# A graph-attention layer on one Trainium2 core: x loaded before the edge lists, edge keys by broadcast transfers instead of matmuls, and the scores of a head pair in one run of six banks

## The chip, the cores and the metric

The kernel runs on one core of one Trainium2 chip. The metric is device time in microseconds of the slowest core (here the only one); lower is better. A core has TensorE (PE, matmuls), VectorE (DVE), ScalarE (ACT), GpSimd (POOL), SyncE (SP, which here only issues transfers), and 16 transfer engines. Each engine works through its own instructions in order; they meet at semaphores.

## What is computed

A pre-normalised graph attention layer on 384 nodes with 1024 features and 16 heads of 64, all in float32:

```python
h = jnp.maximum(_layernorm(x, axis=-1), 0.0)
q = h @ wq.T + bq;  k = h @ wk.T + bk;  v = h @ wv.T + bv
q2 = (q @ wiq.T + biq).reshape(N, H, D).transpose(1, 0, 2)   # k2, v2 alike
mask = jnp.full((N, N), -jnp.inf)
mask = mask.at[src, dst].set(softplus(edge_type_weights)[edge_type - 1])   # 6528 edges, last one wins
# the diagonal is set to softplus(weights)[3] where no edge has set it
scores = jnp.einsum('hnd,hmd->hnm', q2, k2) * scale + mask[None]
attn = softmax(scores)
out = einsum('hnm,hmd->hnd', attn, v2).transpose(1, 0, 2).reshape(N, 1024)
return x + out @ wo.T + bo
```

## The kernel before

**Number format.** Every large product is made of three fp32r matmuls, high by high, low by high and high by low (`products`, L752 to L760). So each operand is split: ACT copies it to a rounded high part, and DVE or POOL subtracts that from the exact value for the low part. The weights come as 56 slabs of 128 x 1024 float32 (512 KB each) through three raw buffers; SP loads slab s when the low part of slab s - 3 is made (`wait_lo`, L232), ACT splits off the high part (L390), and the low part is made by DVE (L627, slabs 1 up to 37) or POOL (L325, L335: slab 0 in two halves, and from slab 38 on).

**The start.** SP issues the edge rows, the edge columns, then x (tile 0 of 128 nodes in halves, tiles 1 and 2 whole), slabs 0 and 1, the fill of two tables of cells in HBM, slab 2 and so on (L259 to L270). POOL makes constants. DVE turns the edge lists to numbers and computes a key per edge, src * 384 + dst (L514 to L524), then the statistics of x (L591 to L597); POOL takes the power for 1/std (L318), DVE makes the shift (L535), and ACT applies Relu(scale * x + shift) (L417); the last half tile is done by DVE (L605, L609). PE runs 13 warming matmuls (L819), turns h around in 24 transposes (L829), three to a feature block k, and multiplies block k - 2 in between; ACT and DVE split each transposed block (L421, L640) in three PSUM banks used in turn. Between the low parts 3 and 4 DVE makes the values of the edges (`edge_values`, L565 to L583).

**Edges.** When several edges hit the same cell, the last must win. For each of 51 tiles of 128 edges, PE brings the 128 keys as a row to all partitions by one matmul against a selecting column (`keys`, L762, four tiles to a unit and a bank), and DVE compares it with the keys as a column and counts later equal ones (L547). Edges with a later equal one are sent to a dump cell (L556, L559). POOL then scatters the values, one transfer of 128 per tile, in two chains on two tables (L346, L352); each chain's scatters wait for one another. Finally both tables are read back (L362) and DVE joins them to the mask (`build_mask`, L629).

**The projections.** Step s of the main loop deals with slab s + 3 and the output tile of slab s, on ACT (L428 to L450) and on DVE (L647 to L667): DVE takes the comparison of edge unit s + 1, the low part of slab s + 3, then the low part of tile s (L615). PE works through v (tiles 0 to 7), then v2 (8 slabs), q, k (16 tiles), then q2 and k2 by pairs of heads. PE may begin tile t only when DVE's low part of tile t - 2 is done (L787), since two banks take turns.

**The pairs.** For each pair j of heads, PE computes scores in three chunks n of 128 query nodes, both heads side by side (L873, 64 rows of the array each), into four banks used in turn (`score_bank`, L155). Around them it places matmuls of the next q2 and k2 tiles (`filler`), transposes of the previous pair's probabilities (L885, into banks 5 to 7), and their products with v2 (L900, L901), which need the transposed block's high part from ACT (L468) and low part from DVE (L692). The order on PE is: chunks 0 and 1, filler, transposes of head h, filler, values of h, chunk 2, transposes of h + 1, filler, values of h + 1 (L951 to L968). On DVE: the maxima of chunks 0 and 1 (`max_part`, L678, one per head and chunk), the sum for the last head of the pair before (`head_part`, L701), reciprocals (L688), the three pt_lo, and later the two maxima of chunk 2. On ACT: exponentials of chunk 0 (L461), the copy of the finished pair (L454, which waits for that sum), exponentials of chunk 1, three pt_hi, and later those of chunk 2. The output projection is drawn into the last pairs.

Of the kernel before, what the change touches and what calls it, by code (L numbers as in the profile page):

```python
# [12 lines left out]
F32 = mybir.dt.float32  # L13
# [7 lines left out]
P = 128  # L21
N = 384
# [30 lines left out]
WARM = 13  # L53
# [16 lines left out]
def gat_kernel(nc, slabs, x, edge_cols, edge_rows, edge_weights, biases, bo, out):  # L70
    with ExitStack() as ctx:
# [32 lines left out]
        rows_i = sb("rows_i", [P, P], I32)  # L104
        rows = sb("rows", [P, P], F16)
# [13 lines left out]
        select = sb("select", [P, ET], F16)  # L119
# [25 lines left out]

        def cell_rows(c):
# [4 lines left out]
        key_bank = bank[0:2]  # L151
        h_bank = [bank[5], bank[4], bank[7]]
        tile_bank = bank[3:5]
        v2_bank = [bank[5:8], bank[0:3]]
        score_bank = [bank[0], bank[1], bank[7], bank[2]]  # L155
        pt_bank = bank[5:8]
# [10 lines left out]
        edges_in, small_in, y_in = sem("edges_in"), sem("small_in"), sem("y_in")  # L167
        x_half_in = sem("x_half_in")
        x_in = [sem(f"x_in{t}") for t in range(NT)]
        slab_in = [sem(f"slab_in{r}") for r in range(RAW)]  # L170
        const_step, iota_ok, select_ok, above_ok = sem("const_step"), sem("iota_ok"), sem("select_ok"), sem("above_ok")
        dump_ok, ident_ok, fill_ok = sem("dump_ok"), sem("ident_ok"), sem("fill_ok")
        edge_step, rows_ok, keys_done, later_ok, value_ok = (
            sem("edge_step"), sem("rows_ok"), sem("keys_done"), sem("later_ok"), sem("value_ok"))
# [19 lines left out]
        y_ok, out_done, out_ok, stored = sem("y_ok"), sem("out_done"), sem("out_ok"), sem("stored")  # L194

# [28 lines left out]
        def lo_by_vector(s):  # L224

            return 1 <= s < LO_ALL
# [31 lines left out]
        def _(sp_eng):  # L258
            sp_eng.dma_start(rows_i[:], edge_rows).then_inc(edges_in, 16)  # L259
            sp_eng.dma_start(cols_i[:], edge_cols).then_inc(edges_in, 16)  # L260

            sp_eng.dma_start(x_sb[:, 0, 0:HALF], x[0:P, 0:HALF]).then_inc(x_half_in, 16)
            sp_eng.dma_start(x_sb[:, 0, HALF:F], x[0:P, HALF:F]).then_inc(x_in[0], 16)
            for t in range(1, NT):
                sp_eng.dma_start(x_sb[:, t, :], x[t * P:(t + 1) * P, :]).then_inc(x_in[t], 16)
            for s in range(SLABS):
                if s >= RAW:

                    wait_lo(sp_eng, s - RAW)
                sp_eng.dma_start(raw[:, s % RAW, :], slabs[s]).then_inc(slab_in[s % RAW], 16)  # L270
                if s == 1:
                    for c in range(2):
                        sp_eng.wait_ge(fill_ok, c + 1)
                        sp_eng.dma_start(cell_rows(c), prob[:, c]).then_inc(filled, 16)
                if s == Q0 + 2:

                    sp_eng.wait_ge(h_turned, KT)
                    for t in range(NT):
                        sp_eng.dma_start(y[:, t, :], x[t * P:(t + 1) * P, :]).then_inc(y_in, 16)
# [7 lines left out]
        def _(pool):  # L287
# [3 lines left out]
            nc.gpsimd.memset(select[:], 0.0).then_inc(const_step, 1)  # L291
# [8 lines left out]
            pool.wait_ge(const_step, 4)  # L300

            nc.gpsimd.affine_select(out=select[:], in_=select[:], compare_op=ALU.not_equal, fill=float(N),
                                    base=0, pattern=[[-1, ET]], channel_multiplier=1).then_inc(const_step, 1)
            pool.wait_ge(const_step, 5)
            nc.gpsimd.affine_select(out=select[:], in_=select[:], compare_op=ALU.not_equal, fill=1.0,
                                    base=-DST_ROW, pattern=[[-1, ET]], channel_multiplier=1).then_inc(select_ok, 1)
# [13 lines left out]

            def split_lo(s):
# [10 lines left out]
            for b in range(2):  # L332
                half = slice(b * HALF, (b + 1) * HALF)
                pool.wait_ge((half_hi, slab_hi)[b], 1)
                nc.gpsimd.tensor_tensor(w_lo[:, 0, half], raw[:, 0, half], w_hi[:, 0, half].bitcast(F32),  # L335
                                        ALU.subtract).then_inc((half_lo, slab_lo)[b], 1)
# [18 lines left out]

            done = 0
# [28 lines left out]
        def _(act):  # L385
# [18 lines left out]
            act.dma_start(ew[:], edge_weights.rearrange("(a n) -> a n", a=1).to_broadcast([P, 4])).then_inc(small_in, 16)  # L404
            act.dma_start(bias[:], biases).then_inc(small_in, 16)
            act.wait_ge(sp_in, 1)
            nc.scalar.activation(sp[:, 2, :], sp[:, 1, :], ACT.Exp).then_inc(sp_exp, 1)
            act.wait_ge(sp_exp, 1)
            nc.scalar.activation(sp[:, 3, :], sp[:, 2, :], ACT.Ln, bias=1.0).then_inc(sp_ln, 1)

# [16 lines left out]
            act.wait_ge(small_in, 32)  # L427
            for s in range(QK0 + TILES_AHEAD):  # L428
                split_hi(s + AHEAD)
                if s < VV0:  # L430
                    tile_hi_part(s)
# [33 lines left out]
            def pt_hi_part(h, m):  # L465

                act.wait_ge(pt_done, h * NT + m + 1)
                nc.scalar.activation(pt_hi[:, m, :], pt_bank[m][:, 0:N], ACT.Copy).then_inc(pt_hi_ok, 1)  # L468
# [42 lines left out]
        def _(dve):  # L511

            dve.wait_ge(edges_in, 32)
# [502 lines left out]
```

## Time and profile before

| | |
|---|---|
| median of 3 runs | 312.71 us (312.55 to 312.86) |
| the profiled execution | 312.73 us |
| its span, first to last instruction | 311.2 us |
| busy: PE / DVE / ACT / POOL | 297.2 / 182.2 / 154.6 / 148.0 us |
| share of the chain that ended last: PE / DVE / ACT / DMA | 88 / 5 / 3 / 2% |
| bytes moved | 37.5 MB, mean 120 GB/s |

The span is 1.53 us shorter than the time of the same execution; the rest lies around the kernel's instructions. PE is nearly always busy, so where it is not, and what it is busy with, are the two questions to bring to the rows. A slab is used every 4.2 to 4.5 us.

### The profile page before, as it was taken

The numbers are of one execution on the slowest core, as the hardware profiler recorded it, in microseconds if no ns is written. First come the engines' busy times: TensorE is split into PE (matmuls) and PEld (weight loads), VectorE is DVE, ScalarE is ACT, GpSimd is POOL, SyncE is SP. The second block draws the span as 40 slices with busy tenths as digits, with TensorE's granted clock in tenths as the row PEclk, the third lists the DMA queues.
The fourth block names the chain that finished last, engine by engine and source line by source line (L and its number), as shares of the span: only waits on it lengthen the run. The fifth ranks groups of instructions, "written<-read, shape, count | busy, mean of one in ns | idle before, by whom it ended". The sixth has DMA issues, their size and how long they took to land.

```text
span 311.2 us, 4801 instructions
## 1 busy us (share of the span) xinstructions
PE 297.2 (95%) x1744; PEld 271.1 (87%) x1744; DVE 182.2 (59%) x476; ACT 154.6 (50%) x288; POOL 148.0 (48%) x152
## 2 busy tenths in 40 slices
PE   1789999999999999999999999999999999999996
PEld 0478999888899999999999999899999998887885
DVE  4989977755354444444467765656566665656341
ACT  3654623324243333333334676767776868874200
POOL 5332565556364455540000895566574748875000
PEclk9999999999999999999999999999999999999999
DMA  6926444443933444447333041122213031310031
GB/s 195 378 73 195 145 137 135 137 137 115 397 107 127 135 137 135 135 126 261 114 127 135 0 138 67 68 69 67 83 55 123 19 133 31 125 48 2 0 137 67
DMA packets 13639, 37.47 MB, mean 120 GB/s; under 512 B 3248, under 2 KB 4528, under 8 KB 13616
## 3 DMA queue, kind: packets, MB, share of 16 engines
q1 hardware_dynamic: 11312, 35.93, 34.0%
q0 software_dynamic: 2016, 1.21, 1.4%
q8 instruction: 14, 0.23, 0.3%
q14 instruction: 9, 0.07, 0.1%
q10 hardware_dynamic: 288, 0.03, 0.1%
HBM read 34.38 MB, written 2.78 MB: 119 GB/s over the span
## 4 chain that ended last, share of the span: by engine, by line
PE 88%; DVE 5%; ACT 3%; DMA 2%; issue 1%; SPq 1%; POOL 0%
PE bank L756 25%; PE bank L760 24%; PE bank L757 24%; PE bank L885 5%; PE bank L873 4%; PE bank L900 3%; PE bank L901 3%; DMA x_sb<-in_x 2%; DVE a_lo L620 1%; PE bank L768 1%; DVE stats L591 1%; ACT pt_hi L468 0%; DVE w_lo L627 0%; ACT work L475 0%; POOL rstd L318 0%
## 5 line engine op out<-in xcount | busy, mean ns | idle before, releaser
L352 POOL DMA_INDIRECT cells<-value,cell x51 | 56.3, 1104 | 54.8 <-DMA cells<-value,cell 42.1
L756 PE MATMUL bank<-a_hi,w_hi 128*128 128x384 f32 x192 | 65.3, 340 | 1.0 <-DVE w_lo L627 0.9
L760 PE MATMUL bank<-a_lo,w_hi 128*128 128x384 f32 x192 | 64.5, 336 | 1.2 <-DVE a_lo L640 1.2
L390 ACT ACTIVATE w_hi<-raw 128x1024 fp32r<-128x1024 f32 x51 | 53.6, 1056 | 22.5 <-PE bank L760 18.4
L757 PE MATMUL bank<-a_hi,w_lo 128*128 128x384 f32 x192 | 64.2, 334 | 0.0
L627 DVE TENSOR_TENSOR w_lo<-raw,w_hi 128x1024 fp32r<-128x1024 f32 x37 | 45.2, 1224 | 18.8 <-ACT w_hi L390 18.6
L369 POOL TENSOR_SCALAR prob<-prob,row_inv 128x384 f32<-128x384 f32 x36 | 22.8, 637 | 54.7 <-DVE row_inv L688 54.6
L325 POOL TENSOR_TENSOR w_lo<-raw,w_hi 128x1024 fp32r<-128x1024 f32 x14 | 33.5, 2394 | 10.5 <-ACT w_hi L390 10.5
L760 PEld LDWEIGHTS bank<-a_lo,w_hi 128*128 128x128 f32 x192 | 36.0, 188 | 1.9 <-DVE a_lo L640 1.8
L756 PEld LDWEIGHTS bank<-a_hi,w_hi 128*128 128x128 f32 x192 | 36.1, 188 | 1.4 <-DVE w_lo L627 1.1
L757 PEld LDWEIGHTS bank<-a_hi,w_lo 128*128 128x128 f32 x192 | 36.1, 188 | 0.0
L461 ACT ACTIVATE prob<-prob,neg_max 128x384 f32<-128x384 f32 x36 | 21.9, 609 | 15.8 <-DVE neg_max L678 15.8
L395 ACT ACTIVATE b_hi<-bank,bias 128x384 fp32r<-128x384 f32 x16 | 9.3, 580 | 35.5 <-PE bank L760 35.5
L692 DVE TENSOR_TENSOR pt_lo<-bank,pt_hi 128x384 fp32r<-128x384 f32 x48 | 23.8, 552 | 4.0 <-ACT pt_hi L468 4.0
L756 PE MATMUL bank<-c_hi,w_hi 128*128 128x384 f32 x64 | 22.7, 355 | 0.2 <-DVE q_lo L615 0.2
L615 DVE SCALAR_TENSOR_TENSOR b_lo<-bank,bias,b_hi 128x384 fp32r<-128x384 f32 x16 | 9.9, 617 | 21.0 <-ACT b_hi L395 21.0
L756 PE MATMUL bank<-b_hi,w_hi 128*128 128x384 f32 x64 | 22.0, 343 | 0.0
L757 PE MATMUL bank<-c_hi,w_lo 128*128 128x384 f32 x64 | 21.5, 336 | 0.0
L760 PE MATMUL bank<-c_lo,w_hi 128*128 128x384 f32 x64 | 21.5, 336 | 0.0
L760 PE MATMUL bank<-b_lo,w_hi 128*128 128x384 f32 x64 | 21.4, 335 | 0.0
L757 PE MATMUL bank<-b_hi,w_lo 128*128 128x384 f32 x64 | 21.4, 335 | 0.0
L678 DVE CUSTOM_DVE_ANT_0 prob<-bank,work 128x384 f32<-128x384 f32 x36 | 18.6, 550 | 4.1 <-PE bank L873 4.1
(135 smaller groups left out, 615.4 us busy)
## 6 DMA issues: line engine op xcount, KB each, us to landing
raw<-in_slabs SPq DMA_DIRECT2D x56, 512.0 KB, 3.3
x_sb<-in_x SPq DMA_DIRECT2D x5, 512.0 KB, 5.7
out_y<-x_sb SPq DMA_DIRECT2D x5, 256.0 KB, 2.6
cells<-prob SPq DMA_DIRECT2D x2, 576.0 KB, 9.4
cells<-value,cell POOLq DMA_INDIRECT x51, 2.9
work<-cells POOLq DMA_DIRECT2D x1, 576.0 KB, 5.9
prob<-cells POOLq DMA_DIRECT2D x1, 576.0 KB, 6.6
x_sb<-in_x SPq DMA_DIRECT2D x2, 256.0 KB, 3.9
```

The lines of the kernel that those rows point to most:

```text
L325: nc.gpsimd.tensor_tensor(lo, raw[:, s % RAW, :], hi.bitcast(F32), ALU.subtract).then_inc(slab_lo, 1)
L352: nc.gpsimd.indirect_dma_start(out=cells[c][:, :], out_offset=bass.IndirectOffsetOnAxis(ap=cell[:, t:t + 1], axis=0), in_=value[:, t:t + 1 ...
L369: nc.gpsimd.tensor_scalar(probs[j % 2][x][:, n, :], probs[j % 2][x][:, n, :], row_inv[:, j % 2, c:c + 1], 1.0, ALU.mult, ALU.mult).then_in ...
L390: nc.scalar.activation(split_place(s)[0], raw[:, s % RAW, :], ACT.Copy).then_inc(slab_hi, 1)
L461: nc.scalar.activation(probs[j % 2][x][:, n, :], probs[j % 2][x][:, n, :], ACT.Exp, scale=-1.0, bias=neg_max[:, j % 2, c:c + 1], accum_out ...
L627: nc.vector.tensor_tensor(lo, raw[:, s % RAW, :], hi.bitcast(F32), ALU.subtract).then_inc(slab_lo_dve, 1)
L678: nc.vector.tensor_tensor_reduce(out=probs[j % 2][x][:, n, :], in0=score_bank[c % 4][:, 0:N], in1=mask[:, n, :], scale=-SCALE, scalar=3.4e ...
L692: nc.vector.tensor_tensor(pt_lo[:, m, :], pt_bank[m][:, 0:N], pt_hi[:, m, :].bitcast(F32), ALU.subtract).then_inc(pt_lo_ok, 1)
L756: nc.tensor.matmul(psum, w[0], a[0], start=first, stop=False)
L757: nc.tensor.matmul(psum, w[1], a[0], start=False, stop=False)
L760: return nc.tensor.matmul(psum, w[0], a[1], start=False, stop=last)
L885: mm = nc.tensor.transpose(pt_bank[m][:, n * P:(n + 1) * P], probs[h // 2 % 2][h % 2][:, n, m * P:(m + 1) * P], ident[:])
```

## The change

- SP issues x first, in six halves, then slab 0, the edge rows (now two transfers to 51 partitions) and columns, slabs 1 and 2, the fills of the cells.
- DVE's edge work ahead of and among the statistics is gone. The key arithmetic (`edge_keys`) and the values stand in step 0 of the main loop, behind the low part of slab 3, followed by unit 0; each later unit stands one step later than before and at the end of its step. The softplus activations on ACT move too.
- Keys: POOL computes the 51 rows of keys, SP writes them to HBM, and one transfer per slab (slabs 3 to 15) broadcasts the keys of a unit to all partitions in SBUF, in buffers that are free at that time. PE's key matmuls, the constant `select` and its two POOL instructions are gone.
- PE warms up earlier (18 matmuls at the start, then 4, 3 and 2 between), transposes h tile by tile as each becomes ready, in seven banks, and multiplies all of tile 0 behind that. The first half of slab 0's low part goes from POOL to DVE, slab 1's from DVE to POOL.
- In pairs 0 to 6 the three chunks of scores run one behind the other in six banks, and DVE takes all six maxima in one go; the transposes of head h use the banks of chunks that are already read. The last pair keeps the old order.

The diff, cut to its core:

```diff
-WARM = 13
+WARM = [18, 4, 3, 2]
...
+        def score_bank(j, c):
+            return bank[(0, 1, 7, 2, 5, 6)[c] if j < PAIRS - 1 else (0, 1, 7, 2, 0, 1)[c]]
+        def pt_bank(h, m):
+            if h >= H - 4:
+                return bank[5 + m]
+            return bank[((0, 1, 7), (2, 5, 6))[h % 2][m]]
...
         def lo_by_vector(s):
-            return 1 <= s < LO_ALL
+            return 2 <= s < LO_ALL
...
         @block.sync
-            sp_eng.dma_start(rows_i[:], edge_rows).then_inc(edges_in, 16)
-            sp_eng.dma_start(cols_i[:], edge_cols).then_inc(edges_in, 16)
-            sp_eng.dma_start(x_sb[:, 0, 0:HALF], x[0:P, 0:HALF]).then_inc(x_half_in, 16)
-            sp_eng.dma_start(x_sb[:, 0, HALF:F], x[0:P, HALF:F]).then_inc(x_in[0], 16)
-            for t in range(1, NT):
-                sp_eng.dma_start(x_sb[:, t, :], x[t * P:(t + 1) * P, :]).then_inc(x_in[t], 16)
+            for t in range(NT):
+                for b in range(2):
+                    half = slice(b * HALF, (b + 1) * HALF)
+                    sp_eng.dma_start(x_sb[:, t, half], x[t * P:(t + 1) * P, half]).then_inc(x_in[t][b], 16)
+            def load_keys(pos):
+                unit = UNIT_ORDER[pos]
+                part = key_rows[0:1, unit * EG * P:(unit * EG + len(tiles_of(unit))) * P]
+                sp_eng.dma_start(key_copy(pos), part.to_broadcast([P, len(tiles_of(unit)) * P])).then_inc(
+                    keys_in[pos], 16)
             for s in range(SLABS):
                 if s >= RAW:
                     wait_lo(sp_eng, s - RAW)
+                    if s == RAW:
+                        sp_eng.wait_ge(half_lo, 1)
                 sp_eng.dma_start(raw[:, s % RAW, :], slabs[s]).then_inc(slab_in[s % RAW], 16)
-                if s == 1:
+                if s == 0:
+                    for i in range(2):
+                        sp_eng.dma_start(rows_i[:, i, :], edge_rows[i * DST_ROW:i * DST_ROW + ET, :]).then_inc(rows_in, 16)
+                    sp_eng.dma_start(cols_i[:], edge_cols).then_inc(edges_in, 16)
+                if s == 2:
                     for c in range(2):
                         sp_eng.wait_ge(fill_ok, c + 1)
                         sp_eng.dma_start(cell_rows(c), prob[:, c]).then_inc(filled, 16)
+                    sp_eng.wait_ge(key_row_ok, 1)
+                    sp_eng.dma_start(key_rows[0, :].rearrange("(t e) -> t e", e=P), key_row[:]).then_inc(keys_out, 16)
+                if 3 <= s < 3 + GROUPS:
+                    if s == 3:
+                        sp_eng.wait_ge(keys_out, 16)
+                    elif s == 9:
+                        sp_eng.wait_ge(filled, 32)
+                    load_keys(s - 3)
...
         @block.gpsimd
+            pool.wait_ge(rows_in, 32)
+            nc.gpsimd.tensor_copy(rows[:], rows_i[:]).then_inc(rows_ok, 1)
+            pool.wait_ge(rows_ok, 1)
+            nc.gpsimd.tensor_scalar(key_row[:], rows[:, 0, :], float(N), 0.0, ALU.mult, ALU.add).then_inc(rows_ok, 1)
+            pool.wait_ge(rows_ok, 2)
+            nc.gpsimd.tensor_tensor(key_row[:], key_row[:], rows[:, 1, :], ALU.add).then_inc(key_row_ok, 1)
...
+            split_lo(1)
             done = 0
             while done < 2 * CHAIN:
...
         @block.scalar
             for k in range(KT):
                 act.wait_ge(h_turned, k + 1)
-                nc.scalar.activation(a_hi[:, k, :], h_bank[k % 3][:, 0:N], ACT.Copy).then_inc(h_hi, 1)
-                if k == 0:
+                nc.scalar.activation(a_hi[:, k, :], h_bank[k][:, 0:N], ACT.Copy).then_inc(h_hi, 1)
+                if k == 1:
                     first_slab_hi(1)
-            for s in range(1, AHEAD):
+                if k == 4:
+                    split_hi(1)
+            for s in range(2, AHEAD):
                 split_hi(s)
+            act.wait_ge(sp_in, 1)
+            nc.scalar.activation(sp[:, 2, :], sp[:, 1, :], ACT.Exp).then_inc(sp_exp, 1)
...
         @block.vector
                     nc.vector.scalar_tensor_tensor(
-                        junk[:, turn % 2, :], key_bank[pos % 2][:, i * P:(i + 1) * P], key[:, t:t + 1], above[:],
+                        junk[:, turn % 2, :], key_copy(pos)[:, i * P:(i + 1) * P], key[:, t:t + 1], above[:],
                         op0=ALU.is_equal, op1=ALU.mult, accum_out=later[:, t:t + 1]).then_inc(later_ok, 1)
...
-            edge_unit_cells(0)
-            for s in range(1, AHEAD):
+            edge_sign()
+            for s in range(2, AHEAD):
                 split_lo(s)
             for s in range(QK0 + TILES_AHEAD):
-                if s + 1 < GROUPS:
-                    edge_unit(s + 1)
+                if s < 2:
+                    tile_lo_part(s)
                 if lo_by_vector(s + AHEAD):
                     split_lo(s + AHEAD)
                 if s < VV0:
-                    tile_lo_part(s)
+                    if s >= 2:
+                        tile_lo_part(s)
+                    if s == 0:
+                        edge_keys()
+                        edge_values()
+                    edge_unit(s)
                 elif s < Q0:
                     g, k = (s - VV0) // KS, (s - VV0) % KS
+                    if s < GROUPS:
+                        edge_unit(s)
...
                 if j < PAIRS:
                     max_part(j, 0)
                     max_part(j, 1)
+                if j < PAIRS - 1:
+                    max_part(j, 2)
                 if j == 0:
                     y_part(0)
                 if j >= 2:
                     head_part(h - 1)
...
+                if j == PAIRS - 1:
+                    max_part(j, 2)
                 if j < PAIRS:
-                    max_part(j, 2)
                     inv_part(j, 2)
...
         @block.tensor
+            warm(WARM[0])
+            pe.wait_ge(ident_ok, 1)
+            for t in range(NT):
+                pe.wait_ge(h_ok, t + 1)
+                for k in range(KT - 1):
+                    if t == NT - 1 and k == HALF // P:
+                        pe.wait_ge(h_last_ok, 1)
+                    turn_h(k, t)
+                warm(WARM[t + 1])
             for k in range(KT):
+                tile(0, a_hi, a_lo, [k])
+                if k == 0:
+                    for t in range(NT):
+                        turn_h(KT - 1, t)
             for t in range(KT):
                 if t >= 1:
                     tile(t, a_hi, a_lo)
-                keys(t + 2)
...
             def turn_probs(h):
                 pe.wait_ge(prob_ok, chunk_at(h // 2, NT - 1, h % 2) + 1)
+                j = h // 2 + 1
+                if j < PAIRS - 1:
+                    pe.wait_ge(masked, chunk_at(j, *((1, 0), (NT - 1, 1))[h % 2]) + 1)
+                elif j == PAIRS - 1 and h % 2 == 0:
+                    pe.wait_ge(masked, chunk_at(j, 1, 0) + 1)
...
                 if j < PAIRS:
                     scores(j, 0)
                     scores(j, 1)
+                if j < PAIRS - 1:
+                    scores(j, 2)
                 filler(j, 0)
...
-                if j < PAIRS:
+                if j == PAIRS - 1:
                     scores(j, 2)
```

## Rows read from the trace of the kernel before

**Rows 1.** Busy by stretch: span, PE, PEld, DVE, ACT, POOL, clock, DMA share.
```profile
0.00:24.04 24.04, 13.53 (x73) 9.39 (x73) 17.75 (x55) 13.27 (x20) 9.80 (x25) 1.00 0.62 209
24.04:266.40 242.36, 242.19 (x1439) 226.64 (x1441) 144.62 (x378) 125.03 (x234) 122.43 (x116) 1.00 0.37 123
266.40:311.20 44.80, 41.45 (x234) 35.09 (x234) 19.81 (x44) 16.31 (x36) 15.79 (x12) 1.00 0.17 59
```

**Rows 2.** Instructions in time, the start: start, duration, engine, line, op [idle before].
```profile
0.80 0.38 SPq L259 DMA_DIRECT2D rows_i<-in_edge_rows  x1
...
1.71 0.42 SPq L262 DMA_DIRECT2D x_sb<-in_x  x1
...
12.66 0.16 DVE L535 SCALAR_TENSOR_TENSOR shift<-mean_var,rstd 128x1 f32<-128x1 f32 x1 [0.36 <-POOL rstd L318]
...
24.04 0.44 PE L756 MATMUL bank<-a_hi,w_hi 128*128 128x384 f32 x1 [0.93 <-DVE w_lo L627]
```

**Rows 3.** Instructions in time on DVE: edge values, one unit, one step.
```profile
17.60 0.15 DVE L569 TENSOR_TENSOR sp<-sp 128x4 f32<-128x4 f32 x1
...
19.63 0.21 DVE L581 TENSOR_TENSOR value<-live,value_part 128x51 f32<-128x51 f32 x1
...
25.04 0.34 DVE L547 SCALAR_TENSOR_TENSOR junk<-bank,key,above 128x128 bf16<-128x128 f32 x1
...
26.52 1.22 DVE L627 TENSOR_TENSOR w_lo<-raw,w_hi 128x1024 fp32r<-128x1024 f32 x1
27.66 0.61 DVE L615 SCALAR_TENSOR_TENSOR b_lo<-bank,bias,b_hi 128x384 fp32r<-128x384 f32 x1
```

**Rows 4.** The page's groups: busy us, mean ns | idle before; POOL's slabs.
```profile
L325 POOL TENSOR_TENSOR w_lo<-raw,w_hi 128x1024 fp32r<-128x1024 f32 x14 | 33.5, 2394 | 10.5 <-ACT w_hi L390 10.5
```

**Rows 5.** Instructions in time on DVE: low parts of two tiles without keys.
```profile
156.24 0.62 DVE L615 SCALAR_TENSOR_TENSOR c_lo<-bank,bias,c_hi 128x384 fp32r<-128x384 f32 x1 [1.99 <-ACT c_hi L395]
...
160.40 0.62 DVE L615 SCALAR_TENSOR_TENSOR q_lo<-bank,bias,q_hi 128x384 fp32r<-128x384 f32 x1 [1.99 <-ACT q_hi L395]
```

**Rows 6.** The chain that ended last: start, duration, what; keys between tiles.
```profile
28.48 0.24 PE bank L768 x4
32.94 0.24 PE bank L768 x4
```

**Rows 7.** The chain again, in pairs 2 and 3: scores and transposes.
```profile
201.48 0.73 PE bank L873 x6
202.21 1.13 PE bank L885 x9
208.57 1.25 PE bank L873 x12
...
211.58 0.98 PE bank L885 x9
```

**Rows 8.** Instructions in time, pair 3: two maxima, pt_lo, PE's load behind it.
```profile
210.28 0.55 DVE L678 CUSTOM_DVE_ANT_0 prob<-bank,work 128x384 f32<-128x384 f32 x1
...
210.76 0.55 DVE L678 CUSTOM_DVE_ANT_0 work<-bank,work 128x384 f32<-128x384 f32 x1
...
214.08 1.49 DVE L692 TENSOR_TENSOR pt_lo<-bank,pt_hi 128x384 fp32r<-128x384 f32 x3 [0.21 <-ACT pt_hi L468]
...
215.62 0.19 PEld L900 LDWEIGHTS bank<-pt_hi,v 128*128 128x128 f32 x1
```

**Rows 9.** Instructions in time: a scatter beside a subtraction on DVE.
```profile
53.44 1.22 DVE L627 TENSOR_TENSOR w_lo<-raw,w_hi 128x1024 fp32r<-128x1024 f32 x1
53.85 1.64 POOL L352 DMA_INDIRECT cells<-value,cell  x1 [1.55 <-DMA cells<-value,cell]
```

**Rows 10.** Instructions in time: the warming matmuls.
```profile
9.16 4.34 PE L819 MATMUL bank<-iota,select 128*128 128x384 f16 x13 [2.81 <-DVE shift L535]
```

**Rows 11.** Read back of the cells: its issue, its landing (page), mask built.
```profile
137.41 0.83 POOL L362 DMA_DIRECT2D work<-cells  x1 [1.86 <-DMA cells<-value,cell]
...
prob<-cells POOLq DMA_DIRECT2D x1, 576.0 KB, 6.6
...
160.94 1.35 DVE L632 SCALAR_TENSOR_TENSOR prob<-prob,work 128x1152 f32<-128x1152 f32 x1
```

More of the change, by code:

```diff
@@ L144, in gat_kernel, with key_copy @@
         cells = [nc.dram_tensor(f"cells{c}", (N * N + P, 1), F32) for c in range(2)]
+        key_rows = nc.dram_tensor("key_rows", (1, E), F32)
+        def key_copy(pos):
+            first, n = [(work2, 0), (work2, 4), (work2, 8), (work, 0), (work, 4), (work, 8), (prob, 19), (prob, 23),
+                        (prob, 3), (prob, 7), (prob, 11), (prob, 15), (prob, 0)][pos], len(tiles_of(UNIT_ORDER[pos])) * P
+            flat = prob[:, :, :, :].rearrange("p a t n -> p (a t n)") if first[0] is prob else first[0]
+            return flat[:, first[1] * P:first[1] * P + n]
         def cell_rows(c):
@@ L330, in pair_lo_part @@
                                         ALU.subtract).then_inc(head_lo, 1)
[L332 to L336, printed above, removed]
+            half = slice(HALF, F)
+            pool.wait_ge(slab_hi, 1)
+            nc.gpsimd.tensor_tensor(w_lo[:, 0, half], raw[:, 0, half], w_hi[:, 0, half].bitcast(F32),
+                                    ALU.subtract).then_inc(slab_lo, 1)
             def scatter(i, c):
@@ L467, in pt_hi_part @@
                 act.wait_ge(pt_done, h * NT + m + 1)
-                nc.scalar.activation(pt_hi[:, m, :], pt_bank[m][:, 0:N], ACT.Copy).then_inc(pt_hi_ok, 1)
+                nc.scalar.activation(pt_hi[:, m, :], pt_bank(h, m)[:, 0:N], ACT.Copy).then_inc(pt_hi_ok, 1)
             def half_part(h):
@@ L561, in edge_unit @@
             def edge_unit(pos):
-                edge_unit_later(pos, range(len(tiles_of(UNIT_ORDER[pos]))))
+                edge_unit_later(pos)
                 edge_unit_cells(pos)
@@ L760, in products @@
                 return nc.tensor.matmul(psum, w[0], a[1], start=False, stop=last)
-            def keys(pos):
-                tiles = tiles_of(UNIT_ORDER[pos])
-                if pos >= 2:
-                    pe.wait_ge(later_ok, (pos - 1) * EG)
-                for i, t in enumerate(tiles):
-                    mm = nc.tensor.matmul(key_bank[pos % 2][:, i * P:(i + 1) * P],
-                                          select[:, t:t + 1].to_broadcast([P, P]), rows[:], start=True, stop=True)
-                mm.then_inc(keys_done, 1)
             def split_slab(s):
@@ L863, in scores @@
                     pe.wait_ge(tile_lo, 3 * KT + 2 * j + 2)
-                for x in range(2):
-                    at = chunk_at(j, n, x)
-                    if n == 0 and j >= 1:
-                        pe.wait_ge(masked, at - 1)
-                    elif n == NT - 1:
-                        pe.wait_ge(masked, at - 3)
+                    if j >= 1:
+                        pe.wait_ge(masked, chunk_at(j - 1, NT - 1, 1) + 1)
+                if j == PAIRS - 1 and n == NT - 1:
+                    pe.wait_ge(masked, chunk_at(j, 0, 1) + 1)
                 for p, (q, k) in enumerate(((q2_hi, k2_hi), (q2_hi, k2_lo), (q2_lo, k2_hi))):
```

148 lines of the change are left out of this document (61 added, 87 removed).

## The prediction

> **What bounds the kernel now.** I read busy time by stretch first, then the instructions in order of time where TensorE (PE) is not full, then the chain where it is. Between 24.04 and 266.40 us PE is busy 242.19 of 242.36 us [rows 1]: there a PE instruction removed is time won, and a wait added to PE is time lost. Ahead of 24.04 PE stands idle 10.5 us [rows 1], and what sets the end is a relay through other engines. Behind 266.40 it is idle 3.4 us [rows 1]; the change leaves the order of that end alone, so I let it move as a block.
>
> The opening relay: x is issued third, at 1.71; the three normalisations end with the last shift at 12.66 (done at 12.82); tile 1 of the first projection starts at 24.04, having waited 0.93 us for the low part of slab 1, made by VectorE (DVE) [rows 2]. DVE came to it late, having done the edge values among the hand-overs of tile 0 (17.60 to 19.84) [rows 3].
>
> **Part 1, the start (expected: tile 3 begins 5.1 us earlier).** x is now first on SP's queue: its first half is issued near 0.8, where the first edge load stood, instead of at 1.71 [rows 2]. The later halves share the transfer engines as before; that they land about 1 us earlier is an estimate from that issue. DVE has no edge work ahead of the statistics now, nor the comparison between tiles 0 and 1 and behind tile 2. I put the last shift's end at 11.4, 1.4 us earlier (bounds 2 and 0.9, the earlier issue alone).
> From there I replay the new order with the old durations. ScalarE (ACT): the last Relu (0.8) to 12.2, eight copies of h at 0.43, half of slab 0 (0.6) behind the second, slab 1 (1.0) behind the fifth: slab 1's high part is there at 16.3. GpSimd (POOL) now makes its low part, in 2.4 us as its others [rows 4]: 18.7. So tile 1 may start at 18.8 instead of 24.04, and tile 3 two tiles of 4.16 us later (156.24 to 160.40, between the low parts of two tiles without keys [rows 5]), at 27.15. The half of slab 0 that moves from POOL to DVE (about 0.65 us) lies behind x's last half and ahead of the first low part, beside ACT's first two copies: nothing, up to its whole 0.65 if DVE comes to it late.
> The new wait: tile 3 needs DVE's low part of tile 1, and behind the low part of tile 0 DVE now has everything of the edges in one run. In order: low half of slab 2 to 20.05; low part of tile 0 to 21.1 (ACT loads its table for Exp ahead of it); slab 3 to 22.6 (1.14 by the starts at 26.52 and 27.66 [rows 3]); keys, five small instructions, about 1.1; values 2.24; the first unit of comparisons 1.48 (25.04 to 26.52); low part of tile 1, 0.61 [rows 3]: done at 28.0. PE reaches tile 3 ready at 27.15 and starts it at **28.1**. Before, tile 3 started at 32.94 + 0.24 = 33.18 [rows 6]. Gain 5.1 us. Afterwards a step costs DVE 1.14 + 0.53 + 1.48 = 3.15 us against PE's 4.16, so it catches up; at tile 4 it is just in time (low part of tile 2 at 32.2). Bounds: 6.0 if DVE's run is not late and 18.8 sets it; 3 if x gains only its issue slots and the DVE run loses another microsecond.
> SP's queue is passed by new work: the three edge loads behind slab 0, then the fill of the cells, the write of the key row and a wait for it ahead of all key loads, one load per slab from slab 3 to 15. Slab 3 needs its buffer at 15.3, when the key row should have landed; slab 4 is queued behind that wait but waits for POOL to 18.7 anyway. The 3.3 MB of key copies add 60 GB/s to the stretch; each is needed two to three slabs after it is issued. I cost them at nothing; if the cover is gone, slabs 4 and 5 come late (rival D).
>
> **Part 2, keys off PE (2.2 us).** The 128-column matmuls that copied key rows to PSUM vanish. A group of four takes 0.24 [rows 6]; behind tile 3's old start 31 matmuls follow in eight groups: 1.86. Each group also costs a restart, a tile step being 4.46 (28.48 to 32.94 [rows 6]), 0.24 of it keys, against 4.16: 0.06, for the six or seven places 0.35. Sum 2.2 us, all on PE, all in the full stretch. DVE now compares from SBUF instead of PSUM; same element count, so 0.35 us each stays, within 0.05 either way, in slack.
>
> **Part 3, three chunks of scores in one run (0.4 us, not 2.5).** A lone third chunk costs 0.73 and makes the transposes behind it 1.13 instead of 0.98 [rows 7]. Two chunks cost 1.25 [rows 7], so in one run the third adds 1.25 - 0.73 = 0.52. So each of seven pairs gives 0.21 + 0.15 = 0.35 us, **2.5 us** if nothing else moves.
> But something moves. DVE now does six maxima before the sum of the last head, not four: 0.48 more each (210.28 to 210.76 [rows 8]), so that sum, ACT's copy of the pair behind it, the exponentials and pt_hi queued behind that copy, and DVE's three pt_lo from 214.08 all come 0.96 later against the start of the scores. PE comes to its consumer only 0.52 later. And there is no slack: the third pt_lo ends at 214.08 + 1.49 = 215.57 and PE's weight load that needs it stands at 215.62 [rows 8], as in pairs 3 to 6 alike. So PE stalls 0.96 - 0.52 - 0.02 = **0.42 us** in each of pairs 2 to 6, and those steps become 0.07 slower, not 0.35 faster. Pairs 0 and 1 (no head to sum, or 1.5 us of slack) keep their gain, 0.4 and 0.35. Sum: 0.75 - 5 x 0.07 = 0.4 us. Bounds: 2.5 without stall; -0.7 if the stall is 0.64 each, with the weight load exposed after it. The second half of a pair has 0.6 us or more in hand except in pair 6, where it is even. The last pair keeps the old order.
>
> **Sum.** 5.1 + 2.2 + 0.4 = 7.7. Profiled span 311.2 - 7.7 = 303.5; the execution lay 1.53 above its span (312.73), so 305.0; that execution is 0.02 from the median of the three runs, and the median becomes **305.0**.
>
> **Where the Trainium skill speaks against it.** A POOL scatter issued at 53.85 took 1.64 us, while DVE's subtraction of two SBUF operands ran until 54.66 [rows 9]. The Trainium skill's GPSIMD Engine Reference, section Key points, says POOL shares its SBUF interfaces with VectorE, in contention with instructions of two SBUF inputs. The trace agrees. The comparisons get a second SBUF input, so by that rule 51 instructions more can hold a scatter. It changes no term of the sum, but feeds rival C.
>
> **Rivals.**
> A. The run of scores pays in full, since DVE starts its maxima earlier or the stall is hidden: 2.1 us more, 302.9. Against it: the weight load that stands 0.05 behind pt_lo in every such pair. 10%.
> B. PE runs the first tiles slowly. The 13 warming matmuls take 4.34 us, 0.33 each for 384 columns [rows 10], against 4.16 / 24 = 0.17 later, though the granted clock reads 1.00 [rows 1]: nearly the ratio of the levels 1.2 and 2.4 GHz. The new order puts PE's warming earlier and leaves pauses between the transposes of one tile and the next. If tile 0 runs at 0.33 from 13.3, it ends 8 us later, at 21.3, and tile 3 starts at 29.6 instead of 28.1: 306.5. The Trainium skill, TensorE: Matmul & The Clock Gate, Part 1, has the half rate as the state after idling. 15%.
> C. The mask comes late, on the other side. The scatters run one after another to 137.41, where the read back begins; with 0.83 us ahead of the second read and 6.6 to its landing the mask was there at 144.8, and DVE asked for it at 160.94 [rows 11]. Now the first unit of the second chain is ready at 30.6 instead of 26.6, so 148.8, and DVE asks at 153.3. PE is held only once mask and next low part miss its scores, at a landing of 156.0. With scatters slowed by held issues and key loads in their queues it decides from 7.2 us of delay; being slower than before takes 7.2 + 7.7 + 0.6 = 15.5 us, 0.3 for each of 54 scatters; 0.4 each gives 305.0 + 21.6 - 7.2 = 319. The part of that which ends slower: 4%; a small delay that only eats gain is in the range.
> D. The transfers collide: the first tiles wait for x or slabs 3 to 5. Half of part 1 is lost: 307.5. For it: 0.62 mean share of the transfer engines before 24.04 [rows 1]. 14%.
> My forecast, 305.0 within 304.0 to 306.3: 57%.
>
> **Range and chances.** 302.4 to 308.3 takes in the forecast, A, B and D. 0.2%, 0.6 us, is about what a measurement here can tell from no change. Faster 0.93, same 0.03, slower 0.04 (C).
>
> **What would show it.** Right: last shift near 11.4; tile 1 on PE near 18.8; PE waiting at tile 3 for DVE's low part of tile 1 (L615's successor), with keys and values just before it; no matmul between tiles; in pairs 2 to 6 a PE idle of 0.4 ahead of the third pt_hi matmul; a pair step of 14.8. Wrong: the step at 14.4 (A), warm matmul spacing in tile 0 (B), DVE waiting for the mask (C), ACT waiting for slabs (D). Most sensitive is the run of DVE behind tile 0, each microsecond of which is one of the result.

## The result, and the profile after

| | before | after |
|---|---|---|
| median | 312.78 us (312.55 to 312.87, 4 runs of the same call) | 304.71 us (304.46 to 304.87, 4 runs) |
| ratio | | 0.9736, 95% interval 0.9724 to 0.9748 |
| span of the profiled execution | 311.2 us | 302.8 us |

The change makes the kernel 8.1 us faster, by the medians; the forecast was 7.7. The two spans differ by 8.4 us. Where they come from is read at five marks on PE, each the start of an instruction that both kernels have: tile 3 of the first projection, the first scores of pairs 0, 2 and 7, and the end.

| PE mark | before | after | gained by then | in this stretch | forecast |
|---|---|---|---|---|---|
| tile 3 | 32.99 | 27.23 | 5.76 | 5.76 | 5.1 |
| pair 0 | 168.00 | 160.05 | 7.95 | 2.19 | 2.2 |
| pair 2 | 193.71 | 184.76 | 8.95 | 1.00 | 0.75 |
| pair 7 | 266.29 | 257.61 | 8.68 | -0.27 | -0.35 |
| end | 311.21 | 302.77 | 8.44 | -0.24 | 0 |

The forecast's own start of tile 3 before is 33.18, which is where the chain that ended last puts it; the instruction stands at 32.99. By the marks used here its 5.1 is 4.9.

Busy time by stretch of the kernel after, cut at some of these marks (columns as in [rows 1]):

```profile
0.00:13.41 13.41, 9.48 (x48) 5.48 (x49) 7.36 (x19) 5.74 (x7) 6.66 (x22) 1.00 0.84 277
13.41:27.23 13.82, 13.82 (x78) 12.71 (x76) 12.40 (x40) 10.24 (x18) 4.97 (x3) 1.00 0.84 268
27.23:160.05 132.82, 132.82 (x722) 126.78 (x722) 78.17 (x184) 50.49 (x65) 59.46 (x55) 1.00 0.53 175
...
```

The full stretch of PE now begins with its first product at 13.41, where before it began at 24.04 [rows 1]. The instructions in order of time show the relay of the new start:

```profile
4.17 0.69 DVE L633 BATCH_NORM_STATS2 stats<-x_sb 128x6 f32<-128x512 f32 x1 [4.17 <-DMA x_sb<-in_x]
5.64 0.69 DVE L633 BATCH_NORM_STATS2 stats<-x_sb 128x6 f32<-128x512 f32 x1 [0.78 <-DMA x_sb<-in_x]
...
11.18 0.33 DVE L580 SCALAR_TENSOR_TENSOR shift<-mean_var,rstd 128x1 f32<-128x1 f32 x1 [0.66 <-POOL rstd L347]
...
16.33 2.41 POOL L361 TENSOR_TENSOR w_lo<-raw,w_hi 128x1024 fp32r<-128x1024 f32 x1 [0.79 <-ACT w_hi L427]
...
18.79 0.45 PE L805 MATMUL bank<-a_hi,w_hi 128*128 128x384 f32 x1
```

The last shift stands at 11.18 and is done at 11.51, for 12.66 and 12.82 in [rows 2]; POOL's low part of slab 1 ends at 18.74 and tile 1 starts at 18.79. The forecast had 11.4, 18.7 and 18.8. Then the run of DVE behind tile 0, in instructions on DVE, ACT and PE:

```profile
18.99 0.20 ACT L461 ACTIVATE sp<-sp 128x4 f32<-128x4 f32 x1 [0.65 <-DVE sp L575]
19.11 0.57 ACT L432 ACTIVATE b_hi<-bank,bias 128x384 fp32r<-128x384 f32 x1
...
20.02 0.61 DVE L656 SCALAR_TENSOR_TENSOR b_lo<-bank,bias,b_hi 128x384 fp32r<-128x384 f32 x1
...
21.80 0.21 DVE L558 CAST cols<-cols_i 128x102 f32<-128x102 int32 x1
...
24.96 0.35 DVE L592 SCALAR_TENSOR_TENSOR junk<-work,key,above 128x128 bf16<-128x128 f32 x1
...
26.46 0.61 DVE L656 SCALAR_TENSOR_TENSOR b_lo<-bank,bias,b_hi 128x384 fp32r<-128x384 f32 x1
...
27.23 0.40 PE L805 MATMUL bank<-a_hi,w_hi 128*128 128x384 f32 x1
```

From the key arithmetic at 21.80 to the low part of tile 1 at 26.46 DVE works through the keys, the values and unit 0 as forecast. That low part is done at 27.07, and tile 3 starts at 27.23: DVE is just in time, where the forecast had it 0.9 us late.

A pair step in the middle of the run, from the chain that ended last (compare [rows 7]):

```profile
199.69 1.77 PE bank L908 x18
201.46 0.37 PE bank L805
...
203.22 0.98 PE bank L923 x9
...
206.86 0.41 PE bank L938
207.27 0.17 PE bank L939
207.45 0.23 PE bank L938
207.68 0.17 PE bank L939
207.85 0.29 PE bank L938
208.14 0.17 PE bank L939
208.32 0.98 PE bank L923 x9
...
214.54 1.77 PE bank L908 x18
```

Eighteen scores take 1.77, that is 1.25 + 0.52, and both groups of transposes 0.98. The six products with pt (L938, L939) take 208.32 - 206.86 = 1.46 us instead of 1.05 (six times 0.174): here the gain goes back. The forecast's sign for it was an idle of 0.4 us ahead of the third product with pt_hi; instead the time is spread over the three products with pt_hi (L938), which take 0.41, 0.23 and 0.29 by the chain. The profile counts nearly all of this as busy PE; only the spacing shows it. The step is 214.54 - 199.69 = 14.85 us, 14.78 to 14.80 before (193.71 to 208.50 for the first of them).

### The profile page after: what moved, and what is told of

Its sections match the earlier page's. It is cut to its first block, busy times and chain, and to the rows that moved or that the text cites. A ratio compares the mean times of both kernels' runs of the same rounds, so it can differ in the third digit from the quotient of the medians.

```text
span 302.8 us, 4742 instructions
## 1 busy us (share of the span) xinstructions
PE 295.2 (98%) x1707; PEld 270.4 (89%) x1707; DVE 179.8 (59%) x475; ACT 153.4 (51%) x288; POOL 149.3 (49%) x152
## 4 chain that ended last, share of the span: by engine, by line
PE 91%; DVE 3%; ACT 2%; DMA 1%; POOL 1%; issue 1%; SPq 0%
PE bank L805 26%; PE bank L809 25%; PE bank L806 25%; PE bank L923 5%; PE bank L908 4%; PE bank L938 3%; PE bank L939 3%; DMA x_sb<-in_x 1%; DVE a_lo L661 1%; DVE stats L633 1%; POOL rstd L347 1%; DVE prob L724 0%; PE bank L857 0%; ACT pt_hi L510 0%; ACT work L517 0%
## 5 line engine op out<-in xcount | busy, mean ns | idle before, releaser
L388 POOL DMA_INDIRECT cells<-value,cell x51 | 55.6, 1090 | 57.4 <-DMA cells<-value,cell 46.0
L668 DVE TENSOR_TENSOR w_lo<-raw,w_hi 128x1024 fp32r<-128x1024 f32 x36 | 44.0, 1223 | 15.2 <-ACT w_hi L427 14.6
L361 POOL TENSOR_TENSOR w_lo<-raw,w_hi 128x1024 fp32r<-128x1024 f32 x15 | 36.0, 2397 | 8.7 <-ACT w_hi L427 8.7
L809 PE MATMUL bank<-b_lo,w_hi 128*128 128x384 f32 x64 | 21.4, 335 | 0.0
L806 PE MATMUL bank<-b_hi,w_lo 128*128 128x384 f32 x64 | 21.4, 334 | 0.0
```

The source lines that it names most:

```text
L361: nc.gpsimd.tensor_tensor(lo, raw[:, s % RAW, :], hi.bitcast(F32), ALU.subtract).then_inc(slab_lo, 1)
L388: nc.gpsimd.indirect_dma_start(out=cells[c][:, :], out_offset=bass.IndirectOffsetOnAxis(ap=cell[:, t:t + 1], axis=0), in_=value[:, t:t + 1 ...
L668: nc.vector.tensor_tensor(lo, raw[:, s % RAW, :], hi.bitcast(F32), ALU.subtract).then_inc(slab_lo_dve, 1)
L806: nc.tensor.matmul(psum, w[1], a[0], start=False, stop=False)
L809: return nc.tensor.matmul(psum, w[0], a[1], start=False, stop=last)
```

## Experiments: what the run of scores gives, and who takes it back

All ratios are against the kernel before, run in the same call. The theory is the forecast's: the run of scores is worth 0.35 us a pair on PE, and DVE's two extra maxima, by way of ACT's queue, take 0.42 of it back from pair 2 on.

**The start and the keys alone.** The kernel after with the pairs of the kernel before:

```diff
-            return bank[(0, 1, 7, 2, 5, 6)[c] if j < PAIRS - 1 else (0, 1, 7, 2, 0, 1)[c]]
+            return bank[(0, 1, 7, 2, 0, 1)[c]]
...
                     scores(j, 1)
-                if j < PAIRS - 1:
-                    scores(j, 2)
...
-                if j < PAIRS - 1:
-                    max_part(j, 2)
```

> The changed kernel with the old order of the pairs (four score banks, third chunk late, two maxima late). Theory (the run of scores gives 0.35 us a pair on PE and loses 0.42 of it in pairs 2 to 6, because DVE's two extra maxima hold ACT's queue): start and keys carry nearly everything, 7.9 to 8.0 us, so 304.9 to 305.3, at most 0.6 above the changed kernel, with a pair step of 14.78 us. Rival (the run of scores was worth its 2.5 us, and the start less than it seems): 306.5 to 307.

Measured: 304.73 us, ratio 0.9743 (0.9730 to 0.9756), beside 0.9736 (0.9724 to 0.9748) for the whole change: no difference that can be told. Its pair steps are 14.79 (200.63 to 215.42).

**The pairs alone**, on the kernel before:

```diff
-        score_bank = [bank[0], bank[1], bank[7], bank[2]]
-        pt_bank = bank[5:8]
+        def score_bank(j, c):
+            return bank[(0, 1, 7, 2, 5, 6)[c] if j < PAIRS - 1 else (0, 1, 7, 2, 0, 1)[c]]
...
                     scores(j, 1)
+                if j < PAIRS - 1:
+                    scores(j, 2)
...
                     max_part(j, 1)
+                if j < PAIRS - 1:
+                    max_part(j, 2)
```

> The kernel before with the new order of the pairs alone. Theory: 312.3 (0.4 to 0.5 us faster than before), with pair steps of 14.85 us from pair 2 on and PE idle or slow ahead of the third matmul on pt_hi. Rival (the run pays in full): 310.3.

Measured: 312.50 us beside 312.88, ratio 0.9992 (0.9983 to 1.0001), which the interval can't quite tell from none. The steps are 14.85, as in the kernel after (207.46 to 222.31 to 237.16). Both halves agree: the gain is the start's and the keys'.

**DVE's sum ahead of its last two maxima**, in the kernel after:

```diff
                     max_part(j, 1)
-                if j < PAIRS - 1:
-                    max_part(j, 2)
                 if j == 0:
                     y_part(0)
                 if j >= 2:
                     head_part(h - 1)
+                if j < PAIRS - 1:
+                    max_part(j, 2)
```

> The changed kernel with DVE's last two maxima of a pair moved behind the sum for the last head of the pair before (head_part), nothing else. Theory: ACT's copy of the pair and with it pt_hi and pt_lo come 0.96 us earlier against the scores, PE's stall of 0.42 goes in pairs 2 to 6, the step falls to 14.43 and the time by 2.1 us to 302.6. Rival 1 (the third chunk in the run costs PE itself as much as alone, so no order of DVE helps): unchanged, 304.7. Rival 2 (the stall only moves to the transposes of head h + 1, which wait for the last maximum): a step of 14.7 or more, 304 or above.

Measured: 302.11 us, ratio 0.9665 (0.9652 to 0.9678), clear of the kernel after. The steps are 14.40. Instructions of one pair in order of time; its scores start at 198.65:

```profile
201.51 0.56 DVE L747 TENSOR_TENSOR work<-bank,work 64x384 f32<-64x384 f32 x1
202.10 0.52 ACT L496 ACTIVATE a_hi<-work 128x384 fp32r<-128x384 f32 x1 [0.71 <-DVE work L747]
204.23 1.49 DVE L738 TENSOR_TENSOR pt_lo<-bank,pt_hi 128x384 fp32r<-128x384 f32 x3 [0.21 <-ACT pt_hi L510]
```

and the same three in the kernel after, where they start at 199.62:

```profile
203.43 0.56 DVE L747 TENSOR_TENSOR work<-bank,work 64x384 f32<-64x384 f32 x1
...
204.03 0.53 ACT L496 ACTIVATE a_hi<-work 128x384 fp32r<-128x384 f32 x1 [1.67 <-DVE work L747]
...
206.16 1.49 DVE L738 TENSOR_TENSOR pt_lo<-bank,pt_hi 128x384 fp32r<-128x384 f32 x3 [0.21 <-ACT pt_hi L510]
```

Against the start of the scores the sum comes at 2.86 instead of 3.81 us, and pt_lo at 5.58 instead of 6.54: 0.96 earlier, as two maxima of 0.48 [rows 8]. PE's six products then take 1.05. The same work in another order is worth 2.6 us by the medians of the two calls, 2.2 by their ratios (0.9736 to 0.9665). The marks side with the ratios: from the scores of pair 2 to those of pair 7 it takes 70.58 us (184.25 to 254.83) instead of 72.85, 2.27 less, and in this execution pair 0 had begun 0.5 us earlier anyway. Both rivals are out.

**DVE's order left alone, ACT's copy moved** behind its three pt_hi:

```diff
-                if j >= 2:
+                if j >= PAIRS - 1:
                     pair_hi_part(j - 2)
                 if j < PAIRS:
                     exp_part(j, 1)
                 if j >= 1:
                     for m in range(NT):
                         pt_hi_part(h, m)
+                if 2 <= j < PAIRS - 1:
+                    pair_hi_part(j - 2)
```

> The changed kernel with DVE's order left alone (six maxima ahead of the sum) and ACT's copy of the finished pair moved behind its three pt_hi, in pairs 2 to 6. Theory (the 0.96 us reach pt_lo only by way of ACT, whose queue stands behind that copy): pt_hi comes as soon as the transposes are there, DVE is free for pt_lo at about 5.0 us behind the start of the scores, PE needs it at 7; no stall, a step of 14.4, 302.1 to 302.6. Rival (DVE itself is late with pt_lo, since it is busy with the six maxima): a step of 14.7 or more, 304 or above.

Measured: 302.12 us, ratio 0.9655 (0.9642 to 0.9668), steps of 14.40. So it isn't that DVE is too busy for pt_lo. ACT, in order, waited for DVE's sum in front of exponentials whose maxima had been there since 201.97 ([1.67 <-DVE work] above; the exponential started at 204.46). Taking either end of that hand-over out of the way is enough, and it gives the same: 70.58 us from pair 2 to pair 7.

**The pairs with the sum first, on the kernel before.** The pairs' edit above, and then the move of `max_part(j, 2)` behind `head_part(h - 1)`, as in the experiment with DVE's sum first:

```diff
                     max_part(j, 1)
...
                 if j >= 2:
                     head_part(h - 1)
+                if j < PAIRS - 1:
+                    max_part(j, 2)
```

> The kernel before with the new order of the pairs and, on DVE, the sum for the last head ahead of the last two maxima. Theory (the run of scores is worth 0.35 us for each of seven pairs once nothing stalls, and something more at pair 1, where PE no longer waits for the low part of q): a step of 14.4, 2.6 to 3.0 us faster than before, 309.9 to 310.3. Rival (the gain seen with the new start came from the two together): 311.5 or above.

Measured: 310.75 us beside 313.00, ratio 0.9931 (0.9918 to 0.9945), 2.2 us faster. It falls between the theory's 309.9 to 310.3 and the rival's 311.5. The steps are 14.41 (193.31, 207.72, 222.14), so the mechanism is the theory's. By the marks the pairs give 2.9 us: 0.98 up to pair 2 and 1.93 from there to pair 7 (72.58 to 70.65). Two things take from it. From the scores of the last pair to the end it is 45.34 us instead of 44.92, which the theory had left out and the next experiment explains. And in this profiled execution pair 0 starts at 168.58 by the chain, where the kernel before had 168.07 in its own; that 0.5 us is already there at tile 1 (24.53 for 24.04). Why isn't known; that stretch of the two programs is the same, and such starts vary (in the five profiled executions of kernels that are alike up to pair 0 with the new start, it stands at 159.60 to 160.16).

**The last pair's wait.** On top of the sum first, the wait of head 12's transposes for the third maximum goes back ahead of the third block:

```diff
-                elif j == PAIRS - 1 and h % 2 == 0:
-                    pe.wait_ge(masked, chunk_at(j, 1, 0) + 1)
                 for m in range(NT):
+                    if j == PAIRS - 1 and h % 2 == 0 and m == NT - 1:
+                        pe.wait_ge(masked, chunk_at(j, 1, 0) + 1)
```

> As e3_sum_first, and in the last pair the wait of head 12's transposes for the third maximum stands again ahead of the third block of transposes instead of the first. Theory: PE's 0.28 us of idle behind the scores of the last pair goes: 302.3. Rival: that wait is hidden by the end's own chain through ACT and DVE: as e3_sum_first, 302.6.

Measured: 301.57 us, ratio 0.9649 (0.9636 to 0.9662); without that edit 302.11. The intervals overlap, so the times alone don't carry it. The profiles do: from the first scores of the last pair to the end it is 44.68 us (255.16 to 299.84) against 45.10 (254.83 to 299.93). In the kernel after, the wait reads so:

```profile
260.11 1.17 PE L923 MATMUL bank<-ident,prob 128*128 128x128 f32 x9 [0.28 <-DVE neg_max L724]
```

There the transposes start 2.50 us behind the first scores of the pair (257.61 to 260.11); in this kernel it is 2.06 (255.16 to 257.22), as in the kernel before (266.29 to 268.35). So the wait costs 0.44 us from start to start. The row's idle of 0.28 shows less, because the profile's modelled end of the product ahead lies behind the point where the next could start. By its median this kernel is the fastest of the study, 3.5% below the kernel before, though its interval overlaps those of the two above.

## Experiments: the start

**Keys put back on PE.** Matmuls that nobody waits for, at the old places:

```diff
+            def key_load(pos):
+                for i in range(len(tiles_of(UNIT_ORDER[pos]))):
+                    nc.tensor.matmul(bank[pos % 2][:, i * P:(i + 1) * P], above[:], above[:], start=True, stop=True)
...
                     tile(t, a_hi, a_lo)
+                key_load(t + 2)
             for s in range(VV0, Q0):
+                if s + 2 < GROUPS:
+                    key_load(s + 2)
```

> The changed kernel with 47 matmuls of 128 columns put back on PE where 11 units of keys were brought across before (behind tiles 0 to 7, ahead of the first three slabs of v2); nobody waits for them, and they bring constants, so they leave the result alone. Theory (in the full stretch every PE instruction is paid): ten groups behind the start of tile 1, 0.24 each and 0.05 to 0.06 for the restart: plus 2.7 to 2.9, 307.5. Rival (they filled time in which PE waited for slabs anyway): 304.7 to 305.5.

Measured: 307.37 us, ratio 0.9819 (0.9803 to 0.9835): 2.66 us above the kernel after. (The matmuls are 43, not the 47 of the expectation.) Behind the start of tile 1, 39 matmuls of 0.06 us, 2.3 us, and the restarts behind them are paid in full: from there to the scores of pair 0 it takes 144.10 us instead of 141.26, 2.84 more.

**DVE 1.14 us later** behind the edge values:

```diff
                         edge_values()
+                        nc.vector.tensor_tensor(pt_lo[:, :, :].rearrange("p m n -> p (m n)")[:, 0:F], x_sb[:, 0, :], x_sb[:, 1, :],
+                                                ALU.add)
```

> The changed kernel with one subtraction's worth of work more on DVE (a 128 x 1024 sum of two SBUF tensors, 1.14 us, into a tensor not in use yet) behind the edge values of step 0. Theory (the run of DVE behind tile 0 ends within 0.1 us of PE's need at tile 3): tile 3 starts 1.1 us later, so 305.8 to 305.9. Rival (tile 3 is set by PE itself and there is slack): 304.7.

```profile
28.02 0.41 PE L807 MATMUL bank<-a_hi,w_hi 128*128 128x384 f32 x1 [0.95 <-DVE b_lo L656]
```

Measured: 305.66 us, ratio 0.9772 (0.9756 to 0.9788), above the kernel after by 0.95 us by the medians and 1.1 by the ratios. The profile decides: tile 3 starts 9.55 us behind tile 1 (18.47 to 28.02), in the kernel after 8.44 (18.79 to 27.23), 1.11 more. (The row's idle of 0.95 is again less than the delay from start to start.) So the 1.14 us on DVE reach PE almost whole, and there was no slack to speak of: in both kernels tile 3 starts 0.15 to 0.16 us behind the end of that low part.

**No warming matmuls:**

```diff
-WARM = [18, 4, 3, 2]
+WARM = [0, 0, 0, 0]
```

> The changed kernel without any of its 27 warming matmuls. Theory (they bring PE to full rate ahead of tile 0): the matmuls of tile 0 take 0.33 us each instead of 0.17 for most of the tile, tile 1 starts at 20 to 21.3 instead of 18.8, and the time rises by 1 to 2.4: 305.7 to 307.1. Rival (tile 0 is paced by ACT's and DVE's hand-overs, tile 1 by POOL's low part of slab 1 at 18.7, and neither sees PE's rate): 304.7.

Measured: 304.85 us, ratio 0.9740 (0.9723 to 0.9756): no difference. The rival holds, but not for its reason alone. PE's weight loads of the transposes of h, three node tiles one behind the other:

```profile
9.42 1.35 PEld L857 LDWEIGHTS bank<-ident,x_sb 128*128 128x128 f32 x7 [9.42 <-issue]
11.22 1.35 PEld L857 LDWEIGHTS bank<-ident,x_sb 128*128 128x128 f32 x7 [0.45 <-ACT x_sb L449]
12.82 0.80 PEld L857 LDWEIGHTS bank<-ident,x_sb 128*128 128x128 f32 x7 [0.24 <-ACT x_sb L449]
```

In the kernel after each such group takes 0.74 to 0.75. Without warming the first two take 1.8 times as long, though the granted clock reads 1.00 throughout, and the third is nearly back; the products of tile 0 then stand 0.17 apart. So PE, which had stood idle, works at a lower rate first and is out of it after fourteen transposes, before it matters. The Trainium skill's TensorE: Matmul & The Clock Gate, Part 1, has the half rate as the state after idling; the spacing here agrees with it, the granted clock of the profile doesn't show it. Of the two longer groups nothing reaches the end, since the next one waits for ACT anyway: from the first transpose to tile 1 it is 9.80 us (9.45 to 19.25), with warming 9.75 (9.04 to 18.79).

**More scatters.** The last scatter of each chain three times:

```diff
-                t = i - NT if c == 0 else LATE + i
+                t = min(i, CHAIN - 1) - NT if c == 0 else LATE + min(i, CHAIN - 1)
...
-            while done < 2 * CHAIN:
+            while done < 2 * CHAIN + 4:
```

> The changed kernel with the last scatter of each chain done three times (same values to the same cells). The mask landed at 153.3 in the changed kernel. Theory (scatters pace at one per chain and 4.16 us, and PE is held once the mask lands behind about 156): landing at 161.6, PE held 5.6 us: 310.3. Rival (slack is larger, since DVE catches up ahead of the first maxima): below 307.

```profile
156.68 1.36 DVE L673 SCALAR_TENSOR_TENSOR prob<-prob,work 128x1152 f32<-128x1152 f32 x1 [3.89 <-DMA prob<-cells]
...
161.15 0.44 PE L908 MATMUL bank<-k_hi,q_hi 64*128 64x384 f32 x2 [1.30 <-DVE k_lo L656]
```

Measured: 307.58 us, ratio 0.9839 (0.9813 to 0.9865), with its four runs from 305.75 to 308.60. The size was missed: 2.9 us by the medians, 3.2 by the ratios, for 5.6. In the profiled execution (the one at 305.75) the mask landed at 156.7, not at 161.6, and PE was held 1.3 us at its first scores. So the landing from which PE is held is 156.7 - 1.3 = 155.4 by that execution, 156.0 by the forecast. What was wrong is where the chain would end: in this execution the four extra scatters took 7.1 us (140.09 to 147.17) for 8.3, and the one ahead of them stood at 140.09, where the kernel after had it at 141.71. The three slower runs have no trace; that their chains ended later is likely but not shown.

## Why the prediction was right, and where it wasn't

- **Part 1, the start** (5.1 forecast, 5.76 measured). The relay to tile 1 held to 0.1 us. The term that failed is the run of DVE: the forecast let ACT load its table for Exp ahead of the low part of tile 0. The trace has no load there: the Exp activation at 18.99 runs on the set that ACT loaded at 1.71, ahead of its first Relu, and the high part of tile 0 follows at 19.11. DVE's low part starts at 20.02 instead of about 20.5, slab 3's at 20.66 instead of 21.4, and the low part of tile 1 ends at 27.07 instead of 28.0. The two loads around it:

```profile
1.71 1.28 ACT L449 ACT_TABLE_LOAD   x1 [1.71 <-PEq L1050]
...
20.64 1.28 ACT L473 ACT_TABLE_LOAD   x1
```

The second is Ln's. So the low part of tile 0 came 0.5 us ahead of the forecast, and that of slab 3, whose high part is next on ACT, 0.7; the other 0.2 is in the keys and hand-overs behind. The lateness of 0.9 us in the forecast wasn't there. That the run is the next limit stands: 1.14 us more on DVE made tile 3 1.11 later. The 5.76 itself is good to a few tenths: with the new start, tile 3 stands at 26.70 to 27.26 in the six profiled executions that are alike up to there, and with the old one at 32.83 to 33.47 in three.
- **Part 2, the keys** (2.2 and 2.19). From tile 3 to the scores of pair 0 it takes 135.01 to 135.04 us in the three profiled executions with the key matmuls and 132.81 to 132.85 in seven without them, so this is no luck of one pair. Adding matmuls back returned it, with the two groups ahead of tile 3.
- **Part 3, the pairs** (0.4 and 0.49: 1.00 - 0.27 - 0.24). Its two terms held: once nothing stalls a step is 14.40 for 14.79, a gain of 0.39 (0.35 forecast), and the stall is 14.85 - 14.40 = 0.45 (0.42). So pairs 2 to 5 lose 0.07 us a step, 8.95 to 8.67 over four, as worked out; pair 6 loses none. Pairs 0 and 1 gave 1.00 for 0.75. Some 0.2 of that is in pair 1, where PE in the kernel before waited for the low part of q behind two chunks and now has a third to do:

```profile
180.22 0.41 PE L756 MATMUL bank<-c_hi,w_hi 128*128 128x384 f32 x1 [0.17 <-DVE q_lo L615]
```

Missed was the last pair, which the forecast took to keep its old order: its transposes now wait for the third maximum ahead of the first block, 0.44 us. From DVE's last sum to the end it is 2.76 us instead of 2.96, for which no run shows a cause. That the total came out near the forecast is luck: the 0.44 that was missed nearly cancels what pairs 0, 1 and 6 and the end gave beyond it.
- **Rival A** (the run pays in full, 302.9) is what the kernel does once the sum goes first: 302.1. **B** was right that PE starts at a lower rate and wrong on where that lies. **D** came in a small way: ACT waited 1.5 us for slab 5 at 26.68, and PE noticed nothing.
- **Rival C, the mask**, was nearer than the forecast put it. The forecast let it land at 148.8, 4.5 us ahead of DVE's need. It came 0.26 us behind it:

```profile
142.98 0.84 POOL L399 DMA_DIRECT2D work<-cells  x1
146.04 0.78 POOL L399 DMA_DIRECT2D prob<-cells  x1 [2.22 <-DMA cells<-value,cell]
...
153.33 1.36 DVE L673 SCALAR_TENSOR_TENSOR prob<-prob,work 128x1152 f32<-128x1152 f32 x1 [0.26 <-DMA prob<-cells]
```

The second read back starts 7.8 us later than before (138.24), not 4.0. The wrong step was to move the chain of scatters as a block. In seven more profiled executions of kernels with the new start and unchanged scatters the second read stands between 142.5 and 146.6, and in two with the old start and the new pairs at 138.4 and 141.3. The means are 144.5 for eight and 139.3 for three, so the new start moves it by some 5.2 us; the rest of the 7.8 is spread. Who waited for the scatters' landings (us, times), before and after:

```profile
  POOL cells L352: 42.1, 27
  POOL cells L388: 46.0, 27
```

From the third scatter to the 54th it is 105.7 us before and 109.7 after. The scatters themselves take POOL as long (57.0 and 56.7 us in sum), so it isn't the comparison's second SBUF operand that made the chain longer; the waits for landings grew by 3.9. Whether the key loads slowed the landings was not tried. PE is held from a landing near 155.4 on, so the kernel after has some 2 us left. Starting the projections still earlier would meet the mask.

## What to carry to other kernels

When a fused run on the busiest engine hands more work at once to a second engine, look for what stands behind it there and whether a third engine, in order, waits for that in front of ready work: 0.39 us a pair was won on PE and 0.45 lost by way of ACT, and moving one sum ahead of two maxima, or one copy behind three, brought 2.3 us. Price each part by where its consumer stood in the trace before: a weight load that starts 0.05 us behind its operand is a chain at its limit even with PE 100% busy. And after each gain at the start, work out anew when the side chain (here the mask) has to be there.

## What the runs showed of the hardware

- The 18 warming matmuls at the start of the kernel after take 5.40 us, 0.3 each, as the 13 before [rows 10], while the four behind the first transposes take 0.81: the granted clock reads 1.00 in both.
- DVE's comparisons kept their 0.35 us when their first operand moved from PSUM to SBUF.
- Broadcasting a unit of keys to 128 partitions from HBM, 256 KB a time beside the slab loads, took 3.8 to 4.6 us from issue to landing in the median, and neither DVE, which reads them, nor PE waited for one.
- A scatter that POOL issues while DVE subtracts two SBUF operands is held until that is done: of the 19 scatters of the kernel before that began during a slab's subtraction, each ended 0.83 to 0.85 us behind the subtraction's end, up to 1.75 us long, where one beside no subtraction takes 0.96 (28 of 29).
